# Cross-attention and mixture-of-experts layer: the splits of the last two pairs of expert weights, moved from the head into the first group

## The reference

```python
xn = layernorm(x)
q, k = xn @ Wq.T, ctx @ Wq.T ; v = k
x = x + softmax(causal(q @ k.T / sqrt(128))) @ v
xf = layernorm(x).reshape(-1, 128)
gates = softmax(xf @ gate_W)
cw = the two largest gates of each token, normalised to sum 1, zero for the others
out = xf
for e in range(8):
    out = out + cw[:, e:e+1] * (relu(xf @ W1[e] + b1[e]) @ W2[e] + b2[e])
return x + out
```

## Time and profile before

| what | value |
|---|---|
| median of 3 runs | 143.75 us |
| profiled execution, its own time | 143.2 us |
| its span | 141.4 us |
| mean granted clock | 0.976 |
| PE busy | 125.1 us (88%) |
| DVE busy | 104.9 us (74%) |
| ACT busy | 96.2 us (68%) |
| POOL busy | 47.3 us (33%) |

### The profile page before, as it was taken

The page is one execution under the profiler, slowest core; times in us unless marked ns, Lnnn a source line. Parts: engine busy times, 40 slices in busy tenths (PEclk is TensorE's granted clock), DMA queues, the critical chain, the costliest instruction groups (busy, mean ns, idle before and its releaser), DMA issues. The chain is left out here.

```text
span 141.4 us, 3259 instructions
## 1 busy us (share of the span) xinstructions
PE 125.1 (88%) x1165; PEld 92.9 (66%) x1165; DVE 104.9 (74%) x413; ACT 96.2 (68%) x191; POOL 47.3 (33%) x53
## 2 busy tenths in 40 slices
PE   6987079789999699999998799999996999699992
PEld 2774055658786457887875468697864677467781
DVE  1529999998559799476586995885497994978573
ACT  3346354976959486796959476769685848689940
POOL 6380342703033750330127532130336603333500
PEclk9999956999999999999999999999999999999999
DMA  3999900000000000200000001000000002000002
GB/s 107 293 270 270 270 4 5 0 0 2 0 5 0 0 7 0 74 0 5 0 0 0 0 5 53 28 0 0 0 5 2 2 5 74 0 2 5 0 0 74
DMA packets 9872, 5.54 MB, mean 39 GB/s; under 512 B 472, under 2 KB 9856, under 8 KB 9856
## 3 DMA queue, kind: packets, MB, share of 16 engines
q1 hardware_dynamic: 9712, 5.27, 12.9%
q10 hardware_dynamic: 144, 0.07, 0.2%
HBM read 4.28 MB, written 1.05 MB: 38 GB/s over the span
## 5 line engine op out<-in xcount | busy, mean ns | idle before, releaser
L623 POOL TENSOR_TENSOR h_lo<-h,h_hi 128x512 f16<-128x512 f32 x24 | 27.9, 1162 | 67.7 <-ACT h L517 67.7
L517 ACT ACTIVATE h<-psH,b1T 128x512 f32<-128x512 f32 x64 | 43.5, 686 | 3.1 <-PE psH L347 1.8
L790 DVE SCALAR_TENSOR_TENSOR acc<-psY,weight_y,acc 128x128 f32<-128x128 f32 x125 | 35.1, 342 | 5.8 <-PE psY L368 5.3
L516 ACT ACTIVATE h_hi<-psH,b1T 128x512 f16<-128x512 f32 x48 | 33.0, 687 | 9.1 <-PE psH L347 9.0
L774 DVE TENSOR_TENSOR h_lo<-h,h_hi 128x512 f16<-128x512 f32 x24 | 17.3, 721 | 15.2 <-ACT h L517 15.2
L347 PE MATMUL psH<-x_lo,w_hi 128*128 128x512 f16 x62 | 23.8, 384 | 0.4
L343 PE MATMUL psH<-x_hi,w_hi 128*128 128x512 f16 x62 | 23.8, 384 | 0.0
L344 PE MATMUL psH<-x_hi,w_lo 128*128 128x512 f16 x62 | 23.8, 383 | 0.0
L368 PE MATMUL psY<-w_hi,h_hi 128*128 128x128 f16 x192 | 22.7, 219 | 0.0
L368 PE MATMUL psY<-w_lo,h_hi 128*128 128x128 f16 x192 | 22.7, 219 | 0.0
L368 PEld LDWEIGHTS psY<-w_hi,h_hi 128*128 128x128 f16 x192 | 15.4, 98 | 3.3
(11 more groups left out here) (169 smaller groups left out, 184.3 us busy)
## 6 DMA issues: line engine op xcount, KB each, us to landing
w_sb<-in_L_ffn_W_dram SPq DMA_DIRECT2D x8, 256.0 KB, 5.1
x_sb<-in_x_dram SPq DMA_DIRECT2D x1, 768.0 KB, 6.9
ctx_sb<-in_ctx_dram SPq DMA_DIRECT2D x1, 768.0 KB, 6.5
out_dram<-acc SPq DMA_DIRECT2D x3, 256.0 KB, 2.3
x_sb<-in_x_dram SPq DMA_DIRECT2D x1, 256.0 KB, 3.5
ctx_sb<-in_ctx_dram SPq DMA_DIRECT2D x1, 256.0 KB, 3.9
out_dram<-acc SPq DMA_DIRECT2D x2, 128.0 KB, 1.8
wq_sb<-in_L_xattn_Wq_dram ACTq DMA_DIRECT2D x1, 64.0 KB, 2.6
```

Of the source, the lines that this page charges most:

```text
L516: nc.scalar.activation(h_hi[:, C * (e % 2) + c, :], psH[c][:, :], ACT.Relu, bias=bias, scale=scale)
L517: nc.scalar.activation(h[:, C * (e % 2) + c, :], psH[c][:, :], ACT.Relu, bias=bias, scale=scale).then_inc(h_ready, 1)
L623: nc.gpsimd.tensor_tensor(h_lo[:, i, :], h[:, i, :], h_hi[:, i, :], ALU.subtract).then_inc(hlo0_ready, 1)
L790: last = nc.vector.scalar_tensor_tensor(out=o, in0=y, scalar=weight_y[:, t, e:e + 1], in1=o, op0=ALU.mult, op1=ALU.add)
```

## The change

On ACT the two high parts of pair 3 leave the head and go to slot 2 of group 0, that is after the relu of expert 2 and ahead of the copy of the values. On DVE the four low parts of pairs 2 and 3 leave the head: W1 of pair 2 goes to slot 2 of group 0 (ahead of `mask_and_max`), W2 of pair 2 to slot 4 (ahead of `add_expert(0, 2)`), W1 of pair 3 to slot 5 (after `add_b2`), W2 of pair 3 to slot 8 (ahead of `second_norm` of the next group). Nothing is added or removed; no DMA, no instruction of PE, POOL or SP is touched, and the waits of PE are the same.

```diff
+        W1_LO, W2_LO, W_HI = (None, None, 2, 5), (None, None, 4, 8), 2
...
                 steps = [(CAT_T, lambda: cat_out(g))]
                 banks = LOOP_BANKS
+                if g == 0:
+                    steps += [(W_HI, lambda: w1_hi_part(3)), (W_HI, lambda: w2_hi_part(3))]
...
             gate_exps(0)
-            w1_hi_part(3)
-            w2_hi_part(3)
             for g in range(0, GROUPS - 1):
...
                 steps = [(B2_ADD, lambda: add_b2(g))]
+                if g == 0:
+                    for p in range(2, PAIRS):
+                        steps += [(W1_LO[p], lambda p=p: w1_lo_part(p)), (W2_LO[p], lambda p=p: w2_lo_part(p))]
...
             gate_top(0, chain)
-            for p in range(2, PAIRS):
-                w1_lo_part(p)
-                w2_lo_part(p)
             LINKS_BEFORE = chain.count
```

## The result

The changed kernel takes 141.56 us (median of 4 runs, 141.34 to 142.13), the kernel before 143.5 us beside it (4 runs, 142.99 to 143.96): ratio 0.987, 95% interval 0.983 to 0.992. Forecast were 142.8 us and a range from 142.3 to 143.8. It became faster, as said, but by 1.9 us where 0.94 was forecast. Timed again in five rounds it was 141.64 against 143.25 us, ratio 0.9905 (0.987 to 0.994): 1.4 us by the ratio, 1.6 us between the two medians. The profiled execution of the changed kernel took 142.13 us with a span of 140.3, against 143.2 and 141.4 before: 1.07 less. In the two profiled executions the forecast of 0.94 is nearly right; in the medians it is not. The experiments are about that difference.

The account below looks back on a forecast made before the run. The prediction took PE's waits to bound the kernel, with the head ending on ACT's chain into the key product. Its terms, -1.04 + 0.1 = -0.94 us, took the median from 143.75 to 142.8 us, range 142.3 to 143.8.

Parts of the forecast that it names:

- What bounds the kernel: ACT's chain into the key product: Head: PE's key product waits 1.43 us for ACT's ctxT copy, with two weight copies in that chain.
- Two high parts, 1.04: ACT's head: without the two copies, relu and ctxT come 1.04 us earlier, all of it gained.
- Four low parts out of the head, 0: DVE's head: removing 2.42 us of low parts gives nothing, since h_lo waits for ACT's last relu.
- The covers (idle times that take the moved work) in slots 2, 4, 5 and 8: ACT and DVE: idle time takes the moved parts at no loss, except 0.1 us in slot 5.
- The margin of 0.05 before weight_catT: ACT, slot 2: high parts take 1.04 us of 1.09 idle; loss taken as 0, bounds 0 and 0.1.
- 0.1 for the meeting with POOL's h_lo: Slot 5: DVE's low part delays POOL's h_lo, then DVE's h_lo; 0.1 us lost, bounds 0 and 0.14.
- Rival A, the power: Slot 8: POOL's power and DVE's low part lock each other out, about 0.61 us lost, 143.4 us; chance 0.18.
- Rival C, the clock: Gap before xf's transposes grows to 2.4 us, clock falls, some 3 us lost; 147 us, chance 0.06.
- The sum: Whole kernel: -1.04 + 0.1 = -0.94 us, taken from the timed median 143.75 to give 142.8 us.

Follow-up runs that it names:

- one copy: Changed kernel, but the high part of W1 of pair 3 stays in ACT's head; 142.01 us, ratio 0.991 to the kernel before.
- the zeros alone: Kernel before, with six products of zeros on PE in the gap before group 0's key product; 142.89 us, ratio 0.996.
- the kernel with four copies more: Changed kernel with four extra 128x512 copies on ACT into an unread spare tile behind gate_exps(0); 145.25 us.

## Why the prediction was wrong

- *What bounds the kernel: ACT's chain into the key product.* Right: the time from the transposes to the key product changed by exactly what ACT had less or more to do in every profile of the table. The prediction left out that DVE's head times this chain up to the gate's exponential.
- *Two high parts, 1.04.* Right: 10.97 to 9.93. With one of them left in the head, 0.52.
- *Four low parts out of the head, 0.* Right: alone they gave ratio 1.002 (0.998 to 1.005).
- *The covers (idle times that take the moved work) in slots 2, 4, 5 and 8.* All held. The margin of 0.05 before weight_catT was enough.
- *0.1 for the meeting with POOL's h_lo.* POOL's was longer by 0.08 (1.24 against 1.16), as worked out; but DVE's h_lo started at 39.94, 0.03 after the end of ACT's h and before POOL's end at 40.07, and was no longer for it (0.69). In the kernel before it had started 0.10 after the end of ACT's h (40.98, 40.88) and 0.02 after that of POOL's h_lo. So the term was no loss but a gain of 0.07: PE's gap before the next transposes of xf is 1.13 instead of 1.20. Whether POOL held DVE up for these 0.07 us in the kernel before is open.
- *Rival A, the power.* Refuted: 1.32 and 0.68.
- *Rival C, the clock.* The right mechanism at the wrong gap and with the wrong sign. The prediction asked what a growing gap before the transposes of xf (1.20) might do, and never asked it of the gap of 1.43 at the key product, which the change shortens. The clock behind that gap is 1.00 in the one execution that had been profiled. But 28 of 68 timed executions of the kernel before have the lower mean clock, and in the one of these that was profiled the clock fell there, at a price of 1.7 us.
- *The sum.* This is the step that failed. "That execution is below all three timed runs, whose median is 143.75, so for the median I predict 143.75 - 0.94" moved the working of one kind of execution to a median that held the other kind. The term missing is the share of falls times their price: 28 / 68 x 1.7 = 0.7 us. With it the mean should fall by 1.04 + 0.7 = 1.7 us; the means of all executions are 143.29 (68) and 141.66 (10), 1.6 us apart. For one copy it gives 0.52 + 0.7 = 1.2, measured 1.3 (mean 142.02); for the zeros alone 0.7, measured 0.7. The measured 141.56 is 1.24 below the 142.8: 0.25 of that is that the median of the kernel before moved from 143.75 to 143.5, and 1.0 that the gain was larger. Of this 1.0 the falls are 0.7 and the term of 0.1 that didn't come is 0.1; the rest is within the scatter of medians of four. A sign of two kinds of execution was on record: 143.75 and 143.96 beside 143.26 and 143.2. The clocks of those timed runs aren't on record, but in the 68 later ones the times of the two kinds don't overlap (up to 143.28 and from 143.46), so the median of 143.75 was by its time an execution of the kind with the fall.

Open: what length of gap decides. No profiled execution had one between 1.43 and 1.97 us. At one place the length does decide: the kernel before and the kernel with four copies more had the same clock until then (0.56 and 0.54 from 23 to 24 us, 1.00 from 24 on) and their gaps begin at 27.29 and 27.31 us; that of 1.43 us had no fall behind it, that of 2.46 us had one. Whether the same length decides where a gap lies otherwise against the clock's earlier rise isn't shown.

## What to carry to other kernels

When a profiled execution lies outside the timed ones, ask what differs between executions before adding a difference to a median; the mean granted clock of each tells two kinds apart at a glance. A gap of PE costs its own length and perhaps a stretch at half clock behind it; shortening it by 0.52 us was worth 1.3 us here (ratio 0.991, 0.988 to 0.994), as it also took away the falls. Idle PE time that can't be removed can be filled with products of zeros into a free bank: that alone was worth 0.4% in the kernel before.

## What the runs showed of the hardware

- After a gap of 1.97 to 2.46 us within dense work the granted clock fell to about half for some 3 us (0.61 and 0.54 in the two stretches shown), in three profiles of the table; after gaps from 0.25 to 1.43 it did not, in eight. Products of zeros in a gap of some 2.7 us kept it up, in all twelve executions.
- The clock's rise at the very start falls on different work from execution to execution, by the spacing of products (the first transposes of x start 0.22 us apart from 4.88 on in one, 0.43 apart from 5.20 on in the other) and moves the whole head by 1.1 us.
- A GpSimd power of 128x4 beside VectorE's low part of weights (two SBUF inputs) was disturbed as little, and disturbed as little, as the longer one of the earlier trace rows: it took 1.32 us and the low part 0.68 us. A GpSimd subtraction of two SBUF tiles did hold up a small VectorE product of two SBUF tiles: 1.15 us instead of 0.19.
